# One counting operation per group in 23 groups, late modulation inside the first group, and a second key piece on VectorE, in a fused adaLN block

## What is computed

```python
mod = (silu(c) @ wmod).reshape(8, 6, 1, 512)
sa, ca, ga, sb, cb, gb = (mod[:, i] for i in range(6))
ga = (2 * (ga >= 0) - 1) * maximum(abs(ga), 0.25)      # gb likewise
h = layernorm(x) * (1 + ca) + sa
q, k, v = ((h @ W + b).reshape(8, 16, 32, 1024) for W, b in ...)
attn = softmax(einsum('bhdt,bhds->bhts', k, v) * temperature)
x = x + ga * einsum('bhdt,bhts->bhds', q, attn).reshape(8, 1024, 512)
h = layernorm(x) * (1 + cb) + sb
scores = h @ w_router                                   # top 512 of 1024 per batch
u = gelu(h[top] @ W1 + b1) @ W2 + b2
x = x + gb * scatter(h + scatter_add(top, sigmoid(scores[top]) * u))
```

## Time and profile before

| | us |
|---|---|
| median of 3 runs | 2326.59 |
| lowest and highest | 2324.39 and 2330.66 |
| the profiled execution, its own time | 2328.77 |
| its span, first to last instruction | 2327.0 |
| PE busy, DVE busy in it | 2258.0 (97%), 1903.7 (82%) |

### The profile page before, as it was taken

How to read it: one execution, slowest core, us unless ns; L and a number is a source line. 1 busy time by engine, 2 the same in 40 slices (tenths; PEclk the granted TensorE clock), 3 DMA queues, 4 the chain that set the end, 5 groups by cost and what they waited for, 6 DMA issues and landing times.

```text
span 2327.0 us, 35730 instructions
## 1 busy us (share of the span) xinstructions
PE 2258.0 (97%) x12786; PEld 883.2 (38%) x12786; DVE 1903.7 (82%) x2909; ACT 1490.0 (64%) x2622; POOL 1244.4 (53%) x1117
## 2 busy tenths in 40 slices
PE   6999999999999999999999999998999999999998
PEld 3333333333333333333333333332444444444443
DVE  5999999999999999999999999999883653563543
ACT  2888888888888888888888888888321111111110
POOL 5667766677666667666767666672452212302300
PEclk9999999999999999999999999999999999999999
DMA  7333343333343333323333423343331111201200
GB/s 241 82 73 80 78 98 73 78 94 74 82 102 73 75 77 91 85 70 87 76 71 80 103 64 78 84 76 100 118 105 50 38 50 50 56 31 51 59 19 19
DMA packets 121267, 179.83 MB, mean 77 GB/s; under 512 B 43736, under 2 KB 43736, under 8 KB 120576
## 3 DMA queue, kind: packets, MB, share of 16 engines
q1 hardware_dynamic: 111152, 152.03, 26.7%
q0 software_dynamic: 9728, 25.23, 3.5%
q10 hardware_dynamic: 208, 0.28, 0.1%
HBM read 67.18 MB, written 43.16 MB: 47 GB/s over the span
## 4 chain that ended last, share of the span: by engine, by line
PE 68%; DVE 21%; POOL 5%; ACT 3%; issue 2%; DMA 1%; SPq 0%; POOLq 0%; DVEq 0%; ACTq 0%
DVE nmax L1057 15%; PE acc L628 14%; PE sc L579 14%; PE sc L779 12%; PE sc L766 12%; PE pj L603 7%; PE pj L591 7%; POOL x L1395 2%; ACT probs L853 2%; DVE stats L1087 1%; DVE qn L1105 1%; DVE dot_out L1073 1%; PE sc L614 1%; ACT room L831 1%; DVE x L1082 1%
## 5 line engine op out<-in xcount | busy, mean ns | idle before, releaser
L853 ACT ACTIVATE probs<-sc,nmax 128x1024 f32<-128x1024 f32 x1024 | 1138.2, 1116 | 219.6 <-DVE nmax L1057 213.0
L1057 DVE TENSOR_REDUCE nmax<-sc 128x1 f32<-128x1024 f32 x1024 | 1217.5, 1213 | 51.4 <-PE sc L579 47.6
L628 PE MATMUL acc<-probs,qn 128*32 128x512 f32 x4136 | 554.7, 609 | 3.0 <-DVE qn L1105 1.6
L943 ACT ACTIVATE probs<-sc,b_col 128x512 f32<-128x512 f32 x128 | 87.9, 687 | 480.7 <-PE sc L766 444.0
L591 PE MATMUL pj<-room 128*128 128x512 f16 x1500 | 386.7, 380 | 3.2 <-POOL room L1380 3.2
L779 PE MATMUL sc<-room,probs 128*128 128x512 f16 x1536 | 353.5, 380 | 3.3 <-DVE hbuf L1243 3.3
L579 PE MATMUL sc<-room 128*128 128x512 f16 x1024 | 309.1, 384 | 17.6 <-ACT probs L853 16.3
L579 PE MATMUL sc<-stacks 128*128 128x512 f16 x1024 | 309.4, 385 | 16.1 <-ACT probs L853 14.6
L1259 DVE CAST probs<-probs 128x512 f16<-128x512 f32 x128 | 60.7, 474 | 247.4 <-ACT probs L943 216.7
L779 PEld LDWEIGHTS sc<-room,probs 128*128 128x128 f16 x1536 | 150.5, 98 | 185.9 <-DVE probs L1261 3.7
L591 PEld LDWEIGHTS pj<-room 128*128 128x128 f16 x1500 | 146.3, 98 | 183.6 <-ACT room L824 6.9
(11 more groups left out here) (164 smaller groups left out, 2230.7 us busy)
## 6 DMA issues: line engine op xcount, KB each, us to landing
stacks<-room SPq DMA_DIRECT2D x512, 64.0 KB, 2.0
room<-room SPq DMA_DIRECT2D x508, 64.0 KB, 2.0
h_rows<-hbuf SPq DMA_DIRECT2D x132, 128.0 KB
out<-base SPq DMA_DIRECT2D x132, 128.0 KB
room<-in_L_attn_x SPq DMA_DIRECT2D x96, 128.0 KB, 2.8
rows<-mod_rows SPq DMA_DIRECT2D x32, 256.0 KB, 4.3
room<-in_L_ffn_W SPq DMA_DIRECT2D x8, 1024.0 KB, 5.1
probs<-in_L_wmod SPq DMA_DIRECT2D x4, 1024.0 KB, 13.6
```

The source lines that it names most:

```text
L628: mm = nc.tensor.matmul(acc[at:at + DH, :], qn[:, (p // 2) % 2, p % 2, h2, :], probs[:, (2 * p + h2) % PROBS, half * D:(half + 1) * D], st ...
L853: nc.scalar.activation(probs[:, u % PROBS, :], slot(g, ring_at(p, h2)), ACT.Exp, bias=nmax[:, u % PROBS:u % PROBS + 1], accum_out=rsum[:, ...
L943: nc.scalar.activation(g32[:, f % 2, :], ff[f % 2], ACT.Gelu_apprx_tanh, bias=b1_col[:, f:f + 1], scale=1.0 / WS).then_inc(gelu_done, 1)
L1057: nc.vector.tensor_reduce(nmax[:, u % PROBS:u % PROBS + 1], slot(g, ring_at(p, h2)), AX.X, ALU.max, negate=True).then_inc(max_done, 1)
```

## The change

Five edits. (1) Ranking of batch 0: the tie count is a function of its own, and each of the 23 operations has a group of its own, groups 6 to 28, behind pair 12. `weights` and `find_slots` go to pairs 12 and 14 of group 29; the load of the scores goes to group 6, where it waits for a store made in group 5. (2) Late modulation: its 16 matmuls take the place of the first four `products` of group 0 (of zeros), into `acc`; ScalarE moves the result out at pair 3, VectorE bounds the gates at pairs 4 and 5, the rows are stored during group 0 and GpSimd waits for them in group 1. (3) The second key piece of group 0 goes over VectorE, as the value pieces do, and the splits no longer wait for GpSimd's. (4) The head temperatures (L816) come behind ScalarE's first evacuation (L831). (5) Feed-forward, batch 0: half a step's tiles are moved, one weight split from f = 2 to f = 1, and `update_parts(0)` from f = 15 to behind the first split of batch 1.

```diff
-        RANK_FROM = NG - 4 - (2 * TB - 2)
+        RANK_FROM = NG - 3 - COUNTS
-        late_ps = sc[:, 1, 0:D]
+        late_ps = acc[:]
@@ SyncE
             sp.wait_ge(s_wsplit, 4)
-            replicate(0, 0, 2, range(HG // 2))
-            replicate(0, 1, 4, range(1, HG // 2))
-            replicate(0, 0, 2, range(HG // 2, HG))
-            replicate(0, 1, 4, range(HG // 2, HG))
-
-            sp.wait_ge(s_modv, 1)
...
+            sp.wait_ge(first_split, 1)
+            replicate(0, 0, 1, range(HG // 2))
+            sp.wait_ge(first_split, 3)
+            replicate(0, 1, 1, range(1, HG // 2))
+            replicate(0, 0, 1, range(HG // 2, HG))
+            replicate(0, 1, 1, range(HG // 2, HG))
...
                     if g == 0:
+                        if b == 0:
+                            store_modulation()
                         sp.wait_ge(acc_free, b * (GB * SUBS) + 2)
...
-                    if b == RANK_FROM // GB and g == 0:
-                        sp.wait_ge(s_sc, 16 * b)
+                    if b * GB + g == RANK_FROM:
+                        sp.wait_ge(s_sc, 16 * 2)
                         load_scores(0)
@@ TensorE
-            for cc in range(CC):
-                late_modulation(cc)
             pe.wait_ge(s_table, 1)
-            pe.wait_ge(qn_done, 1)
-            pe.wait_ge(kv_evac, 4)
-            products(NQ)
...
+                        if b == 0 and g == 0 and p < LAG:
+                            if p == 0:
+                                pe.wait_ge(kv_evac, 4)
+                                pe.wait_ge(acc_free, 1)
+                            late_modulation(p).then_inc(pv_done, 1)
+                        else:
+                            if b == 0 and g == 0 and p == LAG:
+                                pe.wait_ge(s_modc, 1)
@@ ScalarE
             evac_t(sc[:, 2, :], 1, parts=True)
+            act.wait_ge(s_bk, 2 * 16)
+            for hq in range(HG):
...
+            a.then_inc(s_temp, 1)
             act.wait_ge(s_bias, 2)
-            for kk in range(2):
-                evac_kv(0, kk, kk + 1, None, kv_first[kk])
+            evac_kv(0, 0, 1, None, kv_first[0])
...
-            act.wait_ge(kv_split, 4)
+            act.wait_ge(first_split, 3)
...
+                        if b == 0 and g == 0 and p == LAG - 1:
+                            act.wait_ge(pv_done, LAG)
+                            act.wait_ge(s_one, 2)
+                            nc.scalar.activation(mod_b, late_ps, ACT.Identity, bias=one_row[:, 0:1]).then_inc(s_modc, 1)
                         exp_unit(b, g, p, 0)
@@ VectorE
+            dve.wait_ge(s_bias, 2)
+            first_piece(1)
             dve.wait_ge(s_wsplit, 5)
             nc.vector.scalar_tensor_tensor(out=wq16[:, 1], in0=w_stage[2], scalar=WS, in1=wq16[:, 0],
                                            op0=ALU.mult, op1=ALU.subtract).then_inc(s_wsplit, 1)
-            value_piece(3)
+            dve.wait_ge(s_in, 2 * 16)
+            first_piece(2)
+            first_piece(3)
...
-                if n % 2 == 1:
-                    count_before(nc, dve, r, (n + 1) // 2, only)
-                else:
-                    count_above(nc, dve, r, n // 2, only)
+                t, part = divmod(n + 1, 3)
+                (count_before, count_above, count_ties)[part](nc, dve, r, t, only)
...
                         if p == 3:
+                            if b == 0 and g == 0:
+                                dve.wait_ge(s_modc, 1)
                             gated(b, g - 1, 1)
...
+                        if b == 0 and g == 0 and p in (4, 5):
+                            clamp_gates(p - 4)
...
-                        if p == 8 and 0 <= b * GB + g - RANK_FROM < 2 * TB - 1:
+                        if p == 12 and 0 <= b * GB + g - RANK_FROM < COUNTS:
                             rank_first(b * GB + g - RANK_FROM)
-                        if last and g == 1 and p == 6:
+                        if last and g == 1 and p == 12:
                             weights(slice(0, LAST * TB), 1)
-                        if last and g == 1 and p == 8:
+                        if last and g == 1 and p == 14:
                             dve.wait_ge(s_tok, 3)
                             find_slots(nc, dve, r, r.tokens[:, 0:TB, :], only)
...
-            LOW_AT = {2: 2, 4: 3, 5: 4, 7: 5, 9: 6, 10: 7}
-            TILES_AT = {0: (0, 1), 1: (2, 3), 2: (4,), 3: (5, 6), 4: (7,)}
+            LOW_AT = {1: 2, 4: 3, 5: 4, 7: 5, 9: 6, 10: 7}
+            TILES_AT = {0: (0, 1), 1: (2,), 2: (3, 4), 3: (5, 6), 4: (7,)}
...
-                    if f == (FC - 1 if n + 1 < B else TB):
+                    if n and f == (FC - 1 if n + 1 < B else TB):
                         update_parts(n)
+                    if n == 1 and f == 0:
+                        update_parts(0)
@@ GpSimd
-            for kk in range(2):
-                split_kv(0, kk, kk + 1, kk + 1)
+            split_kv(0, 0, 1, 1)
...
-            pool.wait_ge(s_modst, 4 * 16)
...
+                    if b == 0 and g == 1:
+                        pool.wait_ge(s_modst, 4 * 16)
```

96 lines of the change are left out of this document (51 added, 45 removed).

## The result

The changed kernel takes 2307.7 us (median of 4, 2303.61 to 2308.85) where the kernel before, run beside it, takes 2327.94 (4 runs, 2324.39 to 2330.66): the ratio is 0.9913, 95% interval 0.9896 to 0.993. That is faster by more than the 0.3% a measurement can tell, but 10.2 us above the forecast of 2297.5 and 0.7 above the end of its range.

A forecast was written before the change was run, and what follows sets the result against it. TensorE, busy 97% of the span, was taken as the bound. 2328.77 - 18.0 - 2.2 - 10.3 + 2.5 - 1.1 = 2299.7 for the profiled execution, 2297.5 as median; 8-in-10 range 2290 to 2307.

The forecast's parts named there:

- Ranking, -18.0: Groups 6 to 28: one counting operation a group behind pair 12, 0.76 us free there, cuts 20.5 us to 2.5.
- Slower: Rival: late counts idle TensorE until its clock falls, 3.4 us in each of 23 groups, total 2373; chance 0.02.
- Ties held by GpSimd: Rival at pair 12: every tie count waits for GpSimd, 5 us for the eight, total 2302.3; chance 0.06.
- Group 29, -2.2: Weights and slots moved to pairs 12 and 14 leave 2.0 of 4.2 us; bounds 0 and 4.2.
- The start, -10.3: Prologue: second maximum of group 0 at about 43.8 us against 54.1; bounds -13 to -6.
- I carry 1.0 on: Start: moving the temperatures gives back 0.9 to 4.4 us on ScalarE, of which 1.0 is counted further.
- A wait of VectorE for GpSimd in the prologue: Sign named beforehand that would show the prediction to be wrong.
- a copy lands after 2.3 us at the median: Start: landing time of the stack copies; stacks put at 41 us, 38.9 if 2.3 us held.
- The rival that named this: Start gains half: queue holds stacks back or GpSimd and VectorE collide, 5 us not 10.3, total 2302.8; chance 0.15.
- The removal of the 3.64 us of late modulation: Start: taking TensorE's late modulation at 43.72 us out of the prologue, counted inside the -10.3.
- Group 0, +2.5: What comes back in group 0: 0.7 us for ScalarE's move and 1.8 for the gates; bounds 0 and 5.
- The seam, -1.1: Feed-forward, update_parts(0): the 7.08 us wait for stores ends unchanged, one split gets ahead; bounds 0 and -3.3.

The follow-up runs named there:

- rank_at_8: Changed kernel with the second kept batch's gather issued behind the first scatter, counting operations at pair 8 instead of 12: 2310.28 us, 18.1 below its kernel before.
- before_gather_later: Kernel before with only the gather of the second kept batch's base rows moved behind the first scatter: 2322.04 us against 2327.38, ratio 0.998.
- late_first: Changed kernel with all 32 late-modulation matmuls issued together before the first scores, not eight in each of four product turns: 2304.51 us.
- set 2: Four kernels, gather moved behind the first scatter; the pair: changed kernel so edited, 2300.12 us, and the same with the old start, 2303.62.
- start3: Changed kernel with the later gather, three of four modulation-weight loads and the router row issued behind the first twelve key and value copies: 2298.47 us.
- late_undone: Changed kernel with the later gather, late modulation and gates back ahead of group 0, second key piece still on VectorE: 2298.19 us, before 2327.38.
- rank_only: Kernel before with the ranking edit alone, weights and slots at pairs 12 and 14: 2308.16 us, 20.0 below the kernel before.
- again: The changed kernel measured once more without any edit: 2305.77 us, kernel before 2328.18.
- seam_undone: Changed kernel with its feed-forward tables and the place of update_parts(0) as in the kernel before: 2307.63 us.

## Why the prediction was wrong, step by step

Two steps failed. At the seam, the stores were taken to end VectorE's wait, and the gather of 1 MB issued beside them does: 6.7 us of the 8.7 that the profiled execution is over its forecast. At the start, the copies of the first stacks were put at 41 us by a landing time read from a queue that was nearly empty; the last landed at 43.69, and with the clock that fell in the wait for them start and group 0 are 3.25 us short. The terms one by one:

- **Ranking, -18.0:** right, -18.2, and in the main for its reason. The free 0.76 us at pair 12 are what rank_at_8 gives away. Luck has a small part: 2.7 us of it are the two stretches of low clock of this one trace of before, which the prediction read as the price of the operations ("so 3.4 more" for group 14); against `before_gather_later`, with one such stretch, it is -17.1. The rival "Slower" had the mechanism, and put it on the wrong side of the change. The sizes fit: 0.9 for group 6 (0.9 forecast), 0.5 for a count of 896 columns (0.39), nothing for ties and short counts.
- **Ties held by GpSimd** (a rival): none was; all eight last 0.339 to 0.341 us.
- **Group 29, -2.2:** -1.4 in the trace; pair 14, with the slots, takes 6.25 us. And most of the 1.4 is the stretch of low clock in the group 29 of before: against the 51.41 of `before_gather_later` the new place saves 0.2, so the room there was overrated by 2.
- **Between group 30 and the first gelu, 0:** -1.5 in the trace, and by luck. The stretch takes 104.6 to 105.3 us in the ten traces where TensorE's clock falls once in it and 105.7 to 106.4 in the six where it falls twice, with the old ranking (105.33 in `before_gather_later`) as with the new (106.37 in `late_first`). Before had two falls, the changed kernel one.
- **The start, -10.3:** the first of the two steps that failed: the landing of the first stacks, put at 41 and measured at 43.69. -6.4 in the trace, net of group 0 -4.55, and -3.5 by the pair of medians in set 2, against a forecast of -7.8. Four terms of it were off. (1) "I carry 1.0 on" for the temperatures: VectorE's split of Wv began at 22.59 in place of 22.72, so 0.1. (2) "the second key piece from 25.3" with 1.8 us and "Wq to 29.4" with 2.28: the piece began at 26.06 and took 2.56, and Wq's split lasted 3.24, as GpSimd's split of the first key piece now runs beside it; the value split ended at 35.76 and not at 33.3. The Trainium skill (GPSIMD Engine Reference, "Specifications") has the rule, two SBUF inputs on VectorE against GpSimd's shared interface; the trace agrees here. I had put it to the tie counts, beside which nothing of GpSimd's ran, and for the start only into a bound and a rival. "A wait of VectorE for GpSimd in the prologue" was a sign of being wrong, and this is one in effect. (3) "a copy lands after 2.3 us at the median": most copies of that row were issued when the weights (last landing 35.70) and the router row (39.19) were through or nearly so; the first, issued at 32.82, needed 5.2. Issued 3 us sooner the copies needed 5.0, the first of them 8.6, and landed when they had landed before; start3, which takes 3 MB of weights and the router row out from ahead of them, brings them back to 2.5 and 2.8. The rival that named this, at 5 us for the start in place of 10.3, was given 0.15. The Trainium skill (DMA: Bandwidth & Descriptors, "Queues, rings and completion order") says that each engine takes a ring's descriptors in order, and SyncE's copies fit it, the first landing at 38.33 beside the router row at 38.86; though ScalarE's four copies, on another queue than the weights, took as long (5.1), so the order within one ring is not all of it. (4) TensorE's clock: 5.72 us of idleness, and the granted clock is 0.50 for the 3 us that follow, 1.5 us between the two maxima that no term had.
- **The removal of the 3.64 us of late modulation**, "inside the -10.3": it was read off the chain of before, where it stood on the path, without asking what would be there instead. Behind it lay the copies, the last landing at 42.60 before and at 43.69 now, and late_undone shows that it is worth nothing.
- **Group 0, +2.5:** right in size: +1.9 against before, whose clock stood at 0.50 from 56.4 to 59.6, and +2.8 against rank_only, where it did not (46.61).
- **The seam, -1.1:** the edit's own gain is as forecast: at an equal landing TensorE follows 6.7 us behind the wait instead of 7.8, in three traces against three. What failed is "The stores hang on a chain that the change doesn't shorten, so the 7.08 end at the same time". The stores were no later, but they weren't what ended the wait; the gather was, and its end moved from +87.1 to +92.3 in the profiled execution and +90.0 in the next. Moving those four transfers wins 4.9 us of the second batch in the kernel before and 6.0 to 10.5 in the four traces of kernels with the changed start. What the fall of the clock behind the wait costs, 1.6 us before and 2.7 now, had no term either.
- **The sum:** between the 2299.7 forecast for the profiled execution and its 2308.4 lie 8.7 us: 6.7 at the seam, 3.25 at the start with group 0, 0.8 in group 29, less 1.5 behind it, 0.4 in the first feed-forward batch and 0.2 in the ranking. The medians are 10.2 apart and not 8.7, because the changed kernel's profiled execution lay 0.7 above its median, where 2.18 had been taken off for it. In `again` the seam's part is 2.9 and that of the start with group 0 4.0.

What stays open: whether the gather's slow packets are chance. The wait ended at +87.1, +87.5 and +88.2 in the three traces with the old order at the seam and at +88.7, +90.0 and +92.3 in the three with the new one. Nothing in the traces says why the order of VectorE's work should slow a packet, and seam_undone, the old order in the changed kernel, was not faster but 1.9 us slower than `again`. By the start the six traces part as cleanly, +87.1 and +87.5 with the old against +88.2 to +92.3 with the changed one, so they don't say which of the two moves the end, if either does. Open too is what decides whether the clock falls behind a wait of 2.37 us. And it is open by what way the transfers on SyncE's queue slow the copies on ScalarE's; that they do, start3 shows (the weights and the router row were moved together, so it does not say which).

## What to carry to other kernels

When a wait on the path is removed, ask what would have ended it a moment later, and for a transfer take the landing time of a row with the queue as full as it will then be: copies issued 3 us earlier, into loads that had not drained, landed no sooner. Before costing an edit around a wait on DMA, look at every transfer in flight there and at when its data is used; one that is needed 80 us later can hold a wait on stores that share its engines. A trace of before can hold falls of TensorE's clock that another execution doesn't have: look at the granted clock before a group's excess is put down to the work in it. And small work put on a busy engine is priced by its place: over 23 groups of 48.45 us (the mean of groups 1 to 5) the same 23 operations cost 2 to 2.7 us behind pair 12 and 13.3 behind pair 8.
